# Expert weights in high and low parts: all eight inner slices of the looped outputs split, with two subtractions a block on GpSimd and the output eviction on VectorE

## The reference, cut to what matters

```python
x = h.reshape(512, 512)
probs = softmax(x @ gate_w.T); top2_p, top2_i = top_k(probs, 2)
w = top2_p / top2_p.sum(-1, keepdims=True)
hh = gelu(einsum('nd,edf->nef', x, w1) + b1)        # 14 experts, 512 -> 1024
all_out = einsum('nef,efd->ned', hh, w2) + b2       # 1024 -> 512
moe_out = w[:, 0:1] * all_out[n, top2_i[:, 0]] + w[:, 1:2] * all_out[n, top2_i[:, 1]]
result = clip(x + moe_out, -100, 100)
```

## Time and profile before

| | before |
|---|---|
| median of 3 runs | 431.75 us (430.25 to 432.04) |
| the profiled execution | 431.75 us |
| its span | 430.1 us |
| TensorE busy, instructions | 411.1 us (96%), 3090 |
| TensorE weight loads | 313.3 us (73%) |
| VectorE | 332.1 us (77%), 618 |
| ScalarE | 214.2 us (50%), 369 |
| GpSimd | 60.1 us (14%), 80 |
| HBM read, written | 94.04 MB, 21.23 MB |

### The profile page before, as it was taken

The page is one execution under the profiler, slowest core; times in us unless marked ns, Lnnn a source line. Parts: engine busy times, 40 slices in busy tenths (PEclk is TensorE's granted clock), DMA queues, the critical chain, the costliest instruction groups (busy, mean ns, idle before and its releaser), DMA issues.

```text
span 430.1 us, 8272 instructions
## 1 busy us (share of the span) xinstructions
PE 411.1 (96%) x3090; PEld 313.3 (73%) x3090; DVE 332.1 (77%) x618; ACT 214.2 (50%) x369; POOL 60.1 (14%) x80
## 2 busy tenths in 40 slices
PE   1999999999999999999999979999999999999995
PEld 1566566688898899985568746787777778777783
DVE  4759689966169782449957989899988888988766
ACT  4345225131465343131516333698788887778410
POOL 2130000000432120111102801000000000000152
PEclk9999999999999999999989999999999999999999
DMA  8999697999951450019123579899999999994662
GB/s 291 393 377 360 251 427 307 382 409 407 419 195 26 130 216 2 2 29 414 52 94 154 202 223 366 313 346 375 387 392 379 360 373 381 357 359 197 219 197 98
DMA packets 25006, 116.74 MB, mean 271 GB/s; under 512 B 3286, under 2 KB 3302, under 8 KB 18448
## 3 DMA queue, kind: packets, MB, share of 16 engines
q1 hardware_dynamic: 12448, 92.28, 55.7%
q10 hardware_dynamic: 10448, 19.15, 11.7%
q0 software_dynamic: 2080, 4.90, 3.6%
HBM read 94.04 MB, written 21.23 MB: 268 GB/s over the span
## 4 chain that ended last, share of the span: by engine, by line
PE 82%; DVE 8%; ACT 3%; DMA 2%; POOL 2%; issue 2%; ACTq 0%; DVEq 0%
PE banks L2013 5%; PE banks L2014 5%; PE banks L2015 5%; PE banks L2046 4%; PE banks L1623 4%; PE banks L1627 4%; PE banks L2057 3%; PE banks L2056 3%; PE banks L2055 3%; PE banks L1624 3%; PE banks L1610 3%; PE banks L1664 3%; PE banks L1591 3%; PE banks L1858 3%; PE banks L1734 3%; PE banks L1744 3%
## 5 line engine op out<-in xcount | busy, mean ns | idle before, releaser
L1374 DVE TENSOR_TENSOR w_lo<-w,w_hi 128x1024 fp32r<-128x1024 f32 x48 | 55.5, 1218 | 0.0
L662 ACT ACTIVATE w_hi<-w 128x1024 fp32r<-128x1024 f32 x48 | 47.4, 1095 | 2.4 <-DMA w<-in_w 2.4
L747 ACT ACTIVATE A<-banks,b_sb 128x128 f32<-128x128 f32 x112 | 30.5, 384 | 25.9 <-PE banks L2026 16.4
L2013 PE MATMUL banks<-w_hi,cT_r 128*128 128x512 f32 x100 | 40.1, 401 | 0.0
L2015 PE MATMUL banks<-w_hi,cT_r 128*128 128x512 f32 x100 | 39.0, 390 | 0.0
L2014 PE MATMUL banks<-w_lo,cT_r 128*128 128x512 f32 x100 | 39.0, 390 | 0.0
L1477 DVE COPY A<-banks 128x512 f32<-128x512 f32 x28 | 18.0, 685 | 10.2 <-PE banks L2015 10.2
L858 POOL TENSOR_TENSOR A<-A,hrec 128x1024 f32<-128x1024 f32 x8 | 17.1, 2138 | 61.0 <-DVE hrec L1192 61.0
L900 POOL DMA_DIRECT2D b_sb<-in_b1T x12 | 6.5, 543 | 135.8 <-ACT A L747 120.2
L1623 PE MATMUL banks<-w_lo,A2r 128*128 128x512 f32 x52 | 22.7, 436 | 1.5 <-ACT A2r L529 1.3
L1183 DVE TENSOR_REDUCE hmax<-banks 128x16 f32<-128x1024 f32 x8 | 9.8, 1221 | 18.2 <-PE banks L1809 18.2
(11 more groups left out here) (353 smaller groups left out, 1037.9 us busy)
## 6 DMA issues: line engine op xcount, KB each, us to landing
w<-in_w SPq DMA_DIRECT2D x24, 2048.0 KB, 7.8
rows_dram<-A ACTq DMA_DIRECT2D x1, 14592.0 KB, 50.6
A<-in_ctxT SPq DMA_DIRECT2D x8, 1024.0 KB, 8.8
A<-in_ctx SPq DMA_DIRECT2D x8, 1024.0 KB, 8.6
w<-in_w SPq DMA_DIRECT2D x5, 1024.0 KB, 7.9
w<-in_wlT SPq DMA_DIRECT2D x3, 1024.0 KB, 15.2
wqkv<-in_wqkvT SPq DMA_DIRECT2D x1, 3072.0 KB, 14.9
w<-in_convT SPq DMA_DIRECT2D x1, 3072.0 KB, 13.4
```

Source lines behind the costliest of these rows:

```text
L662: nc.scalar.activation(w1_hi[:, u, k * F:(k + 1) * F], w1[:, u, k * F:(k + 1) * F], ACT.Copy).then_inc(hi_ready, 1)
L747: ins = nc.scalar.activation(hT[:, u, f, :], HT[f // 4][:, tile(f % 4)], ACT.Gelu, bias=b1_sb[:, u, f:f + 1])
L1374: nc.vector.tensor_tensor(w1_lo[:, u, part], w1[:, u, part], w1_hi[:, u, part].bitcast(F32), ALU.subtract).then_inc(lo_ready, 1)
L2013: mm(HP[u][c][:, :], xr[:, 0, u, k, :], high[:, at], start=(i == 0), stop=False)
```

## The change

- G becomes 8: all slices of a looped output are split; `high_w2` makes four pieces (CH = 4), the copy of the hidden rows and `low_h` have 1,024 columns. The fourth high piece lies in the merged tensor of the two bias rows (`bias_rows_r`) and in a free part of `wqkv_lo`.
- `split_output` first does high x high and high x low of all slices (it waits for h_high and, piece by piece, for the low parts), then all low x high (it waits for h_low).
- GpSimd takes over two low parts a block: `low_w1_first` (the first slice of w1) and `low_w2_last` (the last piece of w2). VectorE keeps three and three. `hidden` takes the slices of w1 in the order 1, 2, 3, 0.
- `take_y` (VectorE) empties the output bank in the loop, between `low_w2` and `low_h`; ScalarE's `store_y` only issues the DMA, now after `gelu`.

```diff
@@ -85,7 +85,8 @@
         gate = sb("gate", [P, KT, E])
-        bl_row = sb("bl_row", [P, D]); ob_row = sb("ob_row", [P, D])
+        bias_rows, bias_rows_r = overlaid("bias_rows", "bias_rows_r", [P, 2 * D])
+        bl_row, ob_row = bias_rows[:, 0:D], bias_rows[:, D:2 * D]
         b2_sb, b2_r = overlaid("b2_sb", "b2_r", [ROWS3, D])
@@ -188,11 +189,13 @@
         rank = sb("rank", [P, 2]); rel, inb, ww = (sb(v, [P, 2, 2, NT]) for v in ("rel", "inb", "ww")); lpos = sb("lpos", [P, 2, NT]); lw = sb("lw", [P, 2, NT]); wgot = sb("wgot", [P, 2, NT])
-        G = 3 * FT // 4
+        G = FT
         CH = G // 2
+        POOLED = CH - 1
         c_hi_all = c_hi[:, :, :].rearrange("p k n -> p (k n)")
-        w2_hi = [[A2r[:, 6144:7168], A2r[:, 7168:8192], wqkv_lo_flat[:, 4096:5120]],
-                 [c_hi_all[:, 0:1024], c_hi_all[:, 1024:2048], wqkv_lo_flat[:, 5120:6144]]]
+        w2_hi = [[A2r[:, 6144:7168], A2r[:, 7168:8192], wqkv_lo_flat[:, 4096:5120], bias_rows_r[:, :]],
+                 [c_hi_all[:, 0:1024], c_hi_all[:, 1024:2048], wqkv_lo_flat[:, 5120:6144],
+                  wqkv_lo_flat[:, 3072:4096]]]
         h_hi = [v[:, 0:G * P].rearrange("p (f n) -> p f n", f=G) for v in (A2r[:, 1024:2048], att_r[:, :])]
@@ -287,8 +290,9 @@
         y_taken = sem("y_taken")
-        gelu_half, h_high, h_low = sem("gelu_half"), sem("h_high"), sem("h_low")
+        h_high, h_low = sem("h_high"), sem("h_low")
         w2_high, w2_low = sem("w2_high"), sem("w2_low")
+        pool_w1, pool_w2 = sem("pool_w1"), sem("pool_w2")
@@ -746,11 +750,9 @@
                                                bias=b1_sb[:, u, f:f + 1])
-                    if f == G - 1 and not first:
-                        ins.then_inc(gelu_half, 1)
                 ins.then_inc(gelu_done, 1)
                 if not first:
-                    act.wait_ge(gelu_half, b + 1)
+                    act.wait_ge(gelu_done, b + 1)
                     nc.scalar.activation(h_hi[u], hT[:, u, 0:G, :], ACT.Copy).then_inc(h_high, 1)
@@ -764,12 +766,8 @@
-            def store_y(b, u, turn=None):
+            def store_y(b, u):
                 row = rows_of(act, b)
-                if turn is not None:
-                    act.wait_ge(y_psum, b + 3)
-                    act.wait_ge(y_free[u], 16 * turn)
-                    nc.scalar.activation(ysb[:, u, :], YP[:, :], ACT.Copy).then_inc(y_taken, 1)
                 act.wait_ge(y_taken, b + 2)
@@ -781,7 +779,7 @@
             gelu(1, 1, 16, True)
-            for count, n in ((gelu_half, 2), (h_high, 2), (w2_high, 2 * CH)):
+            for count, n in ((h_high, 2), (w2_high, 2 * CH)):
                 act.sem_inc(count, n)
@@ -795,11 +793,11 @@
                         high_w2(2 * i, 0, 16 * i + 16)
-                    store_y(2 * i - 2 + u, u, i)
                     if u == 0:
...
                         gelu(2 * i, 0, 16 * i + 16)
+                    store_y(2 * i - 2 + u, u)
             last = act.value_load(pairs_i[0:1, 1:2], min_val=E // 2 - 1, max_val=MAX_BLOCKS // 2 - 1)
@@ -893,12 +891,33 @@
             pairs = pair_count(pool)
-            with pool.Fori(1, pairs) as i:
+            def low_w1_first(b, u):
+                pool.wait_ge(hi_ready, KT * b + 1)
+                nc.gpsimd.tensor_tensor(w1_lo[:, u, 0:F], w1[:, u, 0:F], w1_hi[:, u, 0:F].bitcast(F32),
+                                        ALU.subtract).then_inc(pool_w1, 1)
+            def low_w2_last(b, u):
+                pool.wait_ge(w2_high, CH * b + CH)
+                at = slice(2 * POOLED * D, 2 * CH * D)
+                nc.gpsimd.tensor_tensor(w2_lo[:, u, at], w2[:, u, at], w2_hi[u][POOLED].bitcast(F32),
+                                        ALU.subtract).then_inc(pool_w2, 1)
+            for u in range(2):
+                pool.wait_ge(gelu_done, u + 1)
+                pool.dma_start(b1_sb[:, u, :], t["b1T"][2 + u]).then_inc(b1_in[u], 16)
+            pool.sem_inc(pool_w1, 4)
+            pool.sem_inc(pool_w2, 2)
+            low_w2_last(2, 0)
+            with pool.Fori(2, pairs) as i:
                 for u in range(2):
...
                         .then_inc(b1_in[u], 16)
+                    low_w1_first(2 * i + u, u)
+                    low_w2_last(2 * i + u - 1, 1 - u)
             pool.wait_ge(y_free[0], 16 * pairs)
@@ -1498,7 +1517,7 @@
-                for i in range(CH):
+                for i in range(POOLED):
                     dve.wait_ge(w2_high, CH * b + i + 1)
@@ -1534,7 +1553,7 @@
                                     ALU.subtract).then_inc(wselT_psum, 1)
-            for count, n in ((h_low, 2), (w2_low, 2 * CH)):
+            for count, n in ((h_low, 2), (w2_low, 2 * POOLED)):
                 dve.sem_inc(count, n)
@@ -1543,8 +1562,9 @@
                     take_xT(2 * i + u, u)
-                    split_lo(2 * i + u, u, range(KT))
+                    split_lo(2 * i + u, u, range(1, KT), 1)
                     low_w2(2 * i + u - 1, 1 - u)
+                    take_y(2 * i + u - 2, u, i)
                     low_h(2 * i + u - 1, 1 - u)
@@ -2004,7 +2024,12 @@
                     i += done
-                    pe.wait_ge(lo_ready, KT * b + i + 1)
+                    if isinstance(b, int):
+                        pe.wait_ge(lo_ready, KT * b + i + 1)
+                    elif k:
+                        pe.wait_ge(lo_ready, (KT - 1) * b + KT + i + 1)
+                    else:
+                        pe.wait_ge(pool_w1, b + 1)
                     part = slice(k * F, (k + 1) * F)
@@ -2042,18 +2067,21 @@
             def split_output(onto, b, u, at, width, between=None):
-                for f in range(G, FT):
-                    mm(onto, hT[:, u, f, :], w2[:, u, f * D + at:f * D + at + width], start=(f == G), stop=False)
-                if between:
-                    between()
+                pe.wait_ge(h_high, b + 1)
+                for f in range(G):
+                    if f == 2 * POOLED:
+                        pe.wait_ge(pool_w2, b + 1)
+                    elif f % 2 == 0:
+                        pe.wait_ge(w2_low, POOLED * b + f // 2 + 1)
+                    if between and f == G // 2:
+                        between()
+                    cols = slice(f * D + at, f * D + at + width)
+                    own = slice(f % 2 * D + at, f % 2 * D + at + width)
+                    mm(onto, h_hi[u][:, f, :], w2_hi[u][f // 2][:, own], start=(f == 0), stop=False)
+                    mm(onto, h_hi[u][:, f, :], w2_lo[:, u, cols], start=False, stop=False)
                 pe.wait_ge(h_low, b + 1)
                 for f in range(G):
-                    if f % 2 == 0:
-                        pe.wait_ge(w2_low, CH * b + f // 2 + 1)
-                    cols = slice(f * D + at, f * D + at + width)
                     own = slice(f % 2 * D + at, f % 2 * D + at + width)
-                    mm(onto, h_hi[u][:, f, :], w2_hi[u][f // 2][:, own], start=False, stop=False)
-                    mm(onto, h_hi[u][:, f, :], w2_lo[:, u, cols], start=False, stop=False)
                     ins = mm(onto, h_lo[:, u, f, :], w2_hi[u][f // 2][:, own], start=False, stop=(f == G - 1))
@@ -2099,7 +2127,7 @@
                     turn_hidden(2 * i + u - 1)
-                    hidden(2 * i + u, u)
+                    hidden(2 * i + u, u, (1, 2, 3, 0))
             last = pe.value_load(pairs_i[0:1, 1:2], min_val=E // 2 - 1, max_val=MAX_BLOCKS // 2 - 1)
```

## The result

| | before | after |
|---|---|---|
| median of the runs side by side | 431.86 us (430.25 to 432.04, 4 runs) | 445.25 us (444.13 to 446.45, 4 runs) |
| the profiled execution, its span | 431.75, 430.1 us | 446.14, 444.5 us |
| period of the loop | 12.58 us | 13.80 us (nine periods, 293.38 to 417.55) |

The ratio is 1.0317, with a 95% interval of [1.0296, 1.0338]: slower by 3.2%, where 445.3 us had been forecast. Every ratio in this text is to the kernel before, measured beside it. Two of the twelve runs of experiment 10, 513.23 and 697.38 us, were slow ones; they count in its median and not in its ratio.

What follows compares the result with a forecast made beforehand. TensorE's own work bounds the loop now (12.58 us); after the change VectorE, held by GpSimd, would set 13.7 us. 431.75 + 13.3 (output(12) later) - 0.37 + 0.65 (wait for take_h) = 445.3 us, range 435 to 453.

Steps and rivals of the forecast that it cites:

- TensorE's part: Looped output matmuls: splitting the two plain slices gains 0.37 us a block, so a TensorE-bound block takes 12.21 us.
- The start: First looped output: TensorE stands 1.65 us waiting for h_high, paid once.
- VectorE's part: VectorE's own loop work: loses one split_lo slice, gains take_y and a longer low_h, 11.1 us (11.13) a block.
- GpSimd's price: GpSimd's two subtractions hold VectorE's two-SBUF-operand instructions: 0.38 us for low_w1_first, 2.22 for low_w2_last, a block.
- The duration of 2.40: Length in us of each GpSimd subtraction, taken from L865, a row with the same operation, shapes and types.
- The period: Looped block: 11.13 + 0.38 + 2.22 = 13.7 us, set by VectorE, against 12.58 before.
- The blocking as the cause: In the loop, GpSimd and VectorE working from SBUF together block each other; one GpSimd instruction costs VectorE nearly its length.
- rival 1: Loop: no blocking worth the name, GpSimd's work free, TensorE bound at 12.21, total 429.3 us; chance 0.12, 0.08 of it faster.
- The sum: Whole kernel: output(3) at 292.8, output(12) at 416.5, 13.3 us later than today; 431.75 + 13.3 - 0.37 + 0.65 = 445.3 us.
- Rival 2: Loop: GpSimd's instructions lie mostly beside PSUM reads; two-operand work of 12.75 us is the floor, 435 to 437 us; chance 0.08.
- the DMA share: Sign in the loop: busy share of the DMA engines falls to near 0.88.

Runs made afterwards that it cites:

- experiment 10: Changed kernel with low_w2_last back on VectorE and ScalarE emptying the output bank before gelu; GpSimd keeps low_w1_first: 429.92 us, ratio 0.9968.
- experiment 2: Changed kernel with GpSimd's two subtractions cut to 32 columns and a memset filling the other 992, low parts left out there: 429.59 us, ratio 0.9954.
- experiment 11: As experiment 10, but block 2's fourth high piece of w2 comes after gelu and the copy, its low part after low_h: 428.95 us, ratio 0.9946.
- Experiment 1: Changed kernel with no subtraction on GpSimd: VectorE makes all eight low parts, hidden takes slices in order 0 to 3: 441.12 us, ratio 1.0216.
- experiment 4: Changed kernel with only low_w2_last back on VectorE; low_w1_first stays on GpSimd: 434.46 us, ratio 1.0092.
- experiment 5: Changed kernel with low_h ahead of take_y and low_w2_last waiting for low_h, to run beside PSUM reads: 443.43 us, ratio 1.0263.
- experiment 6: As experiment 5, with w1's first slice back on VectorE and hidden in order 0 to 3: 441.44 us, ratio 1.0231.
- experiment 9: As experiment 6, but ScalarE issues the store of y one block later, after the next block's split_hi: 432.58 us, ratio 1.0013.

## Why the prediction was right, by its steps

- **TensorE's part**, 12.21 us a block: experiments 2 and 10, in which TensorE is the bound, show 12.27 and 12.26. Right within 0.06.
- **The start**, 1.65 us: TensorE waited 1.66 for h_high. Right, and experiment 11 got most of it back (0.27 left, and 0.37 a block later).
- **VectorE's part**, 11.13 us: after has it only with GpSimd's holds in it. Experiment 1, which has no holds, shows 13.3 for the 13.40 that this count gives with two more subtractions, so the count is about 0.08 too high.
- **GpSimd's price.** `low_w2_last`, 2.22: two slices took 2.21 more in the block shown. `low_w1_first`, 0.38: in turn 0.4 and 0.7, in after as in experiment 4, 0.55 on average. The prediction had it start 1.78 after `take_y` (its terms, 0.7 and 0.98, give 1.68); it starts 1.70 and 1.97 after, because ScalarE begins `split_hi` 0.55 and 0.83 after `take_y` in turn. The duration of 2.40 was right too: 2.41 for w1's, and the 2.53 of w2's has its wait for VectorE in it.
- **The period**, 13.7: measured 13.80. It came out this near because two errors cancel in part: VectorE's own work was put 0.08 too high, and `low_w1_first` 0.17 too low.
- **The blocking as the cause**, against rival 1: shown by experiments 1 and 2 from both sides. Taking the reads away gives rival 1's time (429.59, where 429.3 was worked out); taking GpSimd's help away altogether gives 4 us back. The rule that the Trainium skill has in "SBUF — State Buffer", section "Who interferes with whom", agrees with these runs (3.42 us for 1.22). By the figure of its "GPSIMD Engine Reference", section 3.1, the time would have been about 442; the row's 2.40 was the better one.
- **The sum.** The first looped y let output(3) start at 293.38 for 292.8; nine periods of 13.80 for 13.74 put output(12) at 417.55 for 416.5. The tail from there to the end of the span is 26.95 us, against 430.1 - 403.18 = 26.92 before, where +0.28 had been added: the gathers start 2.85 us after output(12), not 3.8. The errors are +0.6, +0.5 and -0.25, and make up the 0.8 between 445.3 and the profiled 446.14. That the median of four runs is 445.25 is closer than the working deserves: the four lie between 444.13 and 446.45.
- **Rival 2** was given 435 to 437 us as the floor for well placed instructions. The run that placed them (experiment 5) reached 443.4. Its work count was not reached by any run. GpSimd's own queue (the second instruction behind the first and a DMA issue) was left out of it, and so were ScalarE's waits: experiments 5 and 6 show a ring that this rival had no place for.
- **What was wrong**: the DMA share, 0.88 forecast and 0.92 to 0.93 measured. The bytes went as forecast (342 GB/s on average, where the 373 of the earlier trace rows stretched from 12.57 to 13.81 us are 340), but the share didn't fall in step.

## What to carry to other kernels

Before work is handed to an idle GpSimd, count what VectorE reads from SBUF at the same time: here a subtraction of 2.4 us on GpSimd took 2.2 us from VectorE, twice what VectorE needs to do it itself, unless it ran beside reads of PSUM. Placing it there works (the placed instruction cost nothing in experiments 5 to 11), but look at the waits that the placement creates, above all where a store or an eviction ties one engine's order to another's. Here all engines of the loop were within about 1 us of the bound, and opening one ring showed the next wait each time: test each edit alone and keep those that leave the bound where it was.

## What the runs showed of the hardware that was not expected

- A GpSimd instruction that only writes SBUF (a memset, 1.75 us for 1,984 bf16 columns) neither waited for VectorE's subtractions nor held them (experiment 2, which had expected it); one that reads a single operand did both (1.01 us alone, 2.01 beside them, and 2.03 for 1.22 on VectorE).
- The wait is in GpSimd's own record as well: a subtraction of 32 columns took 0.25 us alone and 0.39 to 1.26 beside `low_w2` in experiment 2, so a long GpSimd record may be waiting and not work.
- The DMA engines' busy share was 0.92 at 339 GB/s in after, 0.98 at 383 in experiment 2 and 1.00 at 375 in experiment 4: it didn't follow the bytes, so it didn't tell how much more they could move.
- Loads of 2 MB that took 8.1 us from issue to landing in experiment 10 took 9.4 in experiment 9, with the same bytes and at a period that was longer, not shorter (12.64 us on average for 12.26). Experiment 4, at 12.76 us, has 9.5. The cause is open.
